# A transformer layer with mixture-of-experts on eight cores: Q/K rotation one head behind the projection, one-queue loads of the layer-norm tiles, and the expert activations loaded four tiles at a time

## The chip, the cores and the metric

The kernel runs on the 8 cores of one Trainium2 chip. Each core computes one of 8 sequences of 2048 tokens with a model width of 2048, and there is no exchange between cores. The metric is the device time in microseconds (us) of the slowest core. Lower is better.

## The reference

One pre-norm transformer layer: x + attention(layernorm(x)), and then that plus a feed-forward part of its layer norm. The part that matters:

```python
q = einsum('bsd,dnh->bsnh', x, wq); k = ...wk; v = ...wv     # 16 heads of 128
q = llama_rope(q); k = llama_rope(k); q = q / sqrt(128)
probs = softmax(where(causal, q @ k.T, -1e30)); attn = probs @ v
x = x + einsum('bqnh,nhd->bqd', attn, wo)
h = einsum('th,ehi->eti', ln(x), w1); g = einsum('th,ehi->eti', ln(x), w3)
y_all = einsum('eti,eih->eth', silu(h) * g, w2)              # 8 experts, inner width 1408
y = sum(y_all of the two best experts * their weights)
shared = silu(ln(x) @ sw1) * (ln(x) @ sw3) @ sw2             # inner width 2816
out = x + y + shared
```

## The kernel before

Every instruction is appended to a list per engine by `emit` (L67), in the order of the Python code, with the semaphores that it waits for. What is given to `p.phase` (L64) is added to the waits of every instruction emitted after it. Engines run their lists in order, so the order of the code is the order of work on each engine. DMAs are issued from three queues: SP (`"sync"`), ACT (`"scalar"`) and POOL (`"gpsimd"`). Between the stages stand barriers (`BAR0`, `BAR1`, `BAR2`, `BAR3`, `BAR3B`, `BAR5A`). All matmul operands are bf16. PSUM is used as two halves, `pA` and `pB`, of 128 x 2048 f32 each. The stages:

- **First layer norm** (L354 to L360): 16 tiles of 128 tokens. `load_xt` (L315) loads a tile `xt` of 128 x 2048 f32 (1 MB) in two halves of 512 KB, the left half from the SP queue and the right half from the ACT queue. There are three tile buffers. `emit_ln` (L293) makes two ACT passes (L294, L297), a few tiny DVE and ACT steps, and one DVE pass (L310); `emit_transposes` (L327) makes 16 PE transposes (L334) and 4 ACT copies (L345) into `XLNT`, the transposed activations. The 8 MB weight `WKV` for K is loaded by POOL from the very start (L279).
- **K and Q projections** (L415 to L456): 32 heads one after another through `proj_head` (L377). For each: 64 matmuls of 512 columns into `pA` (L382); an ACT pass that copies `pA` to `kr` (L389); 4 matmuls with a permutation matrix into `pB` (L393), for the rotary embedding; DVE `t1b` = `kr` x cos (L398), `t2b` = `pB` x sin (L401), the sum `krp` (L403); a store from SP. The phase waits of head n hold the ACT pass and the `t2b` of head n-1, so the matmuls of a head begin when both are over. The weights of Q come per head into two buffers `qc` (L428, L453) from the POOL queue, on which the 8 MB load of V's weight into `WKV` (L431) is issued after the last K head.
- **V projection** (L462 to L484), **attention** (L546 to L650), **output projection** (L674 to L705). The change doesn't touch them.
- **Second layer norm** (L778 to L803): as the first, from `X2_sp` in DRAM, with 16 small gate matmuls per tile (L791), an ACT copy of the gate's logits (L798) and the gate's top-2 chain `gate_chain` (L732), which runs one tile behind: it is emitted between the loads of a tile and its ACT passes.
- **Expert part 1** (L854 to L905): 110 blocks (10 experts `pe`, the last two being the shared one, times 11 blocks `ib` of 128 inner columns), each 64 matmuls into `pA` (L861), 64 into `pB` (L876), ACT silu (L868), DVE products (L889, L891 or L896) into `afin`, and a store of 512 KB to the DRAM tensor `AT_sp` (L901). `AT_sp` is laid out [expert, token tile, ib, 128, 128], so each piece of 256 bytes is separate in DRAM.
- **Expert part 2** (L934 to L991): for each half `dh` of the output columns, each expert and each token tile k (2 x 10 x 16 = 320 tiles), a load of 352 KB `asl` from the ACT queue (L951), 22 matmuls (L958), and a DVE addition to `Yacc` (L968 for the first expert, with the residual `x2b` loaded at L947; L975 for the others). There are four `asl` buffers, and a buffer is loaded again when its tile's matmuls are over. The weight `w2s` (2.8 MB in bf16, read as f32, two buffers) of expert pe+1 is loaded from the POOL queue (L925) once the last tile of expert pe-1 is over. The results go out at L982 with the last expert.

## Time and profile before

| what | us |
|---|---|
| time before, median of 2 runs | 7443.65 (7441.2 to 7446.09) |
| time of the profiled execution | 7449.83 |
| span of its slowest core (core 3), from the first to the last instruction | 7448.3 |
| spans of all cores | 7353.9 to 7448.3 |

The span is the time from the first to the last instruction on the core that took longest; 1.5 us lie around it. Stages are told by their place in the span, in us from its start.

### The profile page before, as it was taken

To read this page: it belongs to the slowest core of one execution; us is meant where nothing else is said; L and a number is where in the kernel's file an instruction comes from. 1 tells how busy PE (TensorE), PEld (TensorE's weight loads), DVE (VectorE), ACT (ScalarE), POOL (GpSimd) and SP (SyncE) were. 2 spreads that over 40 slices of the span, in tenths; PEclk is the share of its full clock that TensorE was granted. 3 is DMA by queue.
4 is the path that set the end of the run, shared out by engine and by line. 5 is a ranking of instruction groups with operands and counts; after the bars stand their busy time and mean duration, and the time that the engine had idled before them with its cause. 6 is when DMAs were issued, how large, how long until landed. Compare 5 with 4: busy or idle time off the path is not lost.

```text
span 7448.3 us, 67106 instructions; the slowest of 8 cores (7353.9 to 7448.3 us)
## 1 busy us (share of the span) xinstructions
PE 6335.2 (85%) x28144; PEld 2705.1 (36%) x28144; DVE 1143.7 (15%) x1337; ACT 1051.4 (14%) x1305; POOL 305.9 (4%) x280
## 2 busy tenths in 40 slices
PE   1477788777766259999999999999999799989999
PEld 0232333111122124444444444444444344434444
DVE  1121210111111211111111111111000122222222
ACT  3200012666600320000000000000000000000000
POOL 0000000000000000000000000000000000000000
PEclk9987898777788579999999999999999899999999
DMA  5104313111144325445455455455554655575655
GB/s 109 42 26 79 48 38 68 34 34 34 27 100 95 88 46 60 55 56 60 52 59 60 52 59 60 54 58 60 55 56 54 140 101 114 108 172 118 119 104 129
DMA packets 1295575, 536.24 MB, mean 72 GB/s; under 512 B 1211424, under 2 KB 1219744, under 8 KB 1295280
## 3 DMA queue, kind: packets, MB, share of 16 engines
q0 software_dynamic: 530896, 207.83, 24.4%
q1 hardware_dynamic: 304096, 191.98, 11.3%
q10 hardware_dynamic: 460288, 132.14, 8.0%
q8 instruction: 228, 3.74, 0.2%
q14 instruction: 67, 0.55, 0.0%
HBM read 623.18 MB, written 116.46 MB: 99 GB/s over the span
## 4 chain that ended last, share of the span: by engine, by line
PE 77%; DMA 13%; ACT 5%; DVE 3%; issue 2%; SPq 0%; DVEq 0%; ACTq 0%; POOL 0%; POOLq 0%
PE pB L876 20%; PE pA L861 20%; PE pA L958 9%; PE pB L958 8%; PE pA L382 7%; DMA asl<-AT_sp 5%; DMA xq<-xin 4%; PE pB L609 3%; PE pB L617 2%; PE pA L583 2%; PE pA L471 2%; DMA xt<-xin 1%; PE pB L471 1%; DVE t2b L401 1%; DMA xt<-X_sp 1%
## 5 line engine op out<-in xcount | busy, mean ns | idle before, releaser
L861 PE MATMUL pA<-XLNT,w1c 128*128 128x512 bf16 x7040 | 1540.9, 380 | 2.1 <-ACT beb L845 2.1
L876 PE MATMUL pB<-XLNT,w3c 128*128 128x512 bf16 x7040 | 1541.8, 380 | 0.0
L876 PEld LDWEIGHTS pB<-XLNT,w3c 128*128 128x128 bf16 x7040 | 689.9, 98 | 835.3 <-issue 9.3
L861 PEld LDWEIGHTS pA<-XLNT,w1c 128*128 128x128 bf16 x7040 | 689.2, 98 | 836.5 <-issue 9.2
L958 PE MATMUL pA<-w2s,asl 128*128 128x512 bf16 x3520 | 810.1, 387 | 105.3 <-DMA asl<-AT_sp 105.3
L958 PE MATMUL pB<-w2s,asl 128*128 128x512 bf16 x3520 | 789.2, 380 | 11.3 <-DMA asl<-AT_sp 11.3
L868 ACT ACTIVATE silu<-pA 128x2048 bf16<-128x2048 f32 x110 | 206.5, 1877 | 2811.8 <-PE pA L861 2756.6
L958 PEld LDWEIGHTS pA<-w2s,asl 128*128 128x128 bf16 x3520 | 348.8, 99 | 543.8 <-issue 148.5
L889 DVE TENSOR_TENSOR atmp<-silu,pB 128x2048 bf16<-128x2048 bf16 x88 | 201.3, 2288 | 2150.0 <-PE pB L876 2125.7
L958 PEld LDWEIGHTS pB<-w2s,asl 128*128 128x128 bf16 x3520 | 345.1, 98 | 429.3 <-issue 18.3
L590 ACT ACTIVATE exp<-pA,EXB 128x512 bf16<-128x512 f32 (+3 forms) x544 | 340.9, 640 | 152.1 <-PE pA L583 147.6
L334 PE MATMUL pA<-IDB,sqb 128*128 128x128 bf16 x256 | 32.4, 306 | 372.2 <-DVE sqb L310 372.2
L382 PE MATMUL pA<-XLNT,qc 128*128 128x512 bf16 x1024 | 260.0, 421 | 61.0 <-DVE t2b L401 41.6
L382 PE MATMUL pA<-XLNT,WKV 128*128 128x512 bf16 x1024 | 260.5, 422 | 49.2 <-DVE t2b L401 39.9
L685 PE MATMUL pA<-woq,ATTNT 128*128 128x512 bf16 x768 | 200.1, 422 | 98.4 <-DVE x2q L692 98.4
L975 DVE TENSOR_TENSOR Yacc<-Yacc,pA 128x1024 f32<-128x1024 f32 x144 | 175.9, 1222 | 598.1 <-PE pA L958 598.1
L583 PE MATMUL pA<-qtn,ktn 128*128 128x512 bf16 (+3 forms) x544 | 219.9, 416 | 53.3 <-DVE ATTNT L644 27.2
L975 DVE TENSOR_TENSOR Yacc<-Yacc,pB 128x1024 f32<-128x1024 f32 x144 | 175.9, 1221 | 511.0 <-PE pB L958 495.5
L609 PE MATMUL pB<-exp,ONESC 128*1 128x512 bf16 (+3 forms) x640 | 240.4, 376 | 2.5 <-DVE exp L597 0.9
L526 POOL DMA_DIRECT2D w1c<-w x88 | 100.8, 1145 | 2215.8 <-PE pA L861 2215.8
L382 PEld LDWEIGHTS pA<-XLNT,qc 128*128 128x128 bf16 x1024 | 107.7, 106 | 216.7 <-issue 123.3
L382 PEld LDWEIGHTS pA<-XLNT,WKV 128*128 128x128 bf16 x1024 | 107.7, 106 | 204.8 <-issue 110.1
(111 smaller groups left out, 2490.6 us busy)
## 6 DMA issues: line engine op xcount, KB each, us to landing
asl<-AT_sp ACTq DMA_DIRECT2D x320, 352.0 KB, 3.6
AT_sp<-afin SPq DMA_DIRECT2D x110, 512.0 KB, 11.7
w1c<-w POOLq DMA_DIRECT2D x88, 512.0 KB, 9.0
w3c<-w POOLq DMA_DIRECT2D x88, 512.0 KB, 13.5
w2s<-w POOLq DMA_DIRECT2D x16, 2816.0 KB, 22.5
xq<-xin SPq DMA_DIRECT2D x64, 256.0 KB, 4.6
X_sp<-x2q SPq DMA_DIRECT2D x64, 256.0 KB, 3.6
x2b<-X_sp SPq DMA_DIRECT2D x32, 512.0 KB, 6.0
```

The costliest lines, as they stand in the source:

```text
L382: emit("tensor", lambda e, db=db, c=c, lcol=lcol, lhs_tile=lhs_tile: e.matmul(pA[:, c * 512:(c + 1) * 512], lhs_tile[:, lcol:lcol + 128], ...
L471: emit("tensor", lambda e, db=db, c=c, ps=ps, i=i: e.matmul(ps[:, c * 512:(c + 1) * 512], XLNT[:, db * 2048 + i * 128: db * 2048 + (i + 1) ...
L583: sps=sps, soff=soff: e.matmul(sps[:, soff:soff + b - a], ktn[par][:, j * 128:(j + 1) * 128], qtn[par][:, q0 + a:q0 + b], start=True, stop ...
L590: sps=sps, soff=soff: e.activation(expt[my_epar][:, 0:b - a], sps[:, soff:soff + b - a], AF.Exp, bias=EXB[:, 0:1]),
L609: stz=first_z[bank], gsp=grp_stop: e.matmul(pB[0:1, a:b], ONESC[:, :], expt[my_epar][:, 0:b - a], start=stz, stop=gsp),
L685: emit("tensor", lambda e, nb=nb, i=i, pcol=pcol, wbuf=wbuf: e.matmul(pA[:, pcol:pcol + 512], ATTNT[:, nb * 2048 + i * 128: nb * 2048 + (i ...
L861: emit("tensor", lambda e, db=db, c=c, slot=slot: e.matmul(pA[:, c * 512:(c + 1) * 512], w1c[slot][:, db * 128:(db + 1) * 128], XLNT[:, db ...
L868: tsilu = emit("scalar", lambda e: e.activation(silu[:, :], pA[:, :], AF.Silu), waits=[th, silu_free], inc="s_s")
L876: emit("tensor", lambda e, db=db, c=c, slot=slot: e.matmul(pB[:, c * 512:(c + 1) * 512], w3c[slot][:, db * 128:(db + 1) * 128], XLNT[:, db ...
L889: ta = emit("vector", lambda e: e.tensor_mul(atmp[:, :], silu[:, :], pB[:, :]), waits=[tg2, tsilu], inc="s_v")
L958: psl=psl: e.matmul(psl[0][:, psl[1] + c * 512: psl[1] + (c + 1) * 512], asl[apar][:, ib * 128:(ib + 1) * 128], w2s[pe % 2][:, ib * 1024 + ...
L975: tac = emit("vector", lambda e, k=k, psl=psl: e.tensor_add(Yacc[k][:, :], Yacc[k][:, :], psl[0][:, psl[1]:psl[1] + 1024]), waits=[tmm, ya ...
```

## The change

It has four parts.

1. `load_xt` issues one DMA of 1 MB for the whole tile, from SP alone. Nothing is issued from ACT any more. It is used in both layer norms.
2. `proj_head` is cut in two, `proj_part` (the 64 matmuls and the ACT pass) and `perm_part` (the permutation, the DVE steps, the store). `perm_part` of head h-1 is emitted after `proj_part` of head h. Even heads use `pA` and odd heads `pB`, and the permutation's result overwrites the half that the head's own projection used. The phase of head h waits for the `t2b` of head h-2. The first two `qc` loads are emitted at the start, and V's weight load after the 64 matmuls of the last K head.
3. `AT_sp` is laid out [expert, ib, 128, token], so a store writes 4 KB rows. Expert part 2 loads four token tiles at once, `aslg` of 128 x 11 x 512 bf16 (1408 KB, in rows of 1 KB), into two buffers; a buffer is loaded again when the fourth of its tiles is over. There are 80 loads in place of 320.
4. The first of these loads and the first `x2b` load are issued before the last expert of part 1.

```diff
     V_sp = nc.dram_tensor("V_sp", [S, D], BF16, kind="Internal")
     X2_sp = nc.dram_tensor("X2_sp", [S, D], F32, kind="Internal")
-    AT_sp = nc.dram_tensor("AT_sp", [NPE, NT, NIB, 128, 128], BF16, kind="Internal")
+    AT_sp = nc.dram_tensor("AT_sp", [NPE, NIB, 128, S], BF16, kind="Internal")
     GSP = nc.dram_tensor("GSP", [8, S], F32, kind="Internal")
 
...
     grb = [A("gr0", [1, S], BF16, offset=WB + 36864),
            A("gr1", [1, S], BF16, offset=WB + 40960)]
 
-    asl = [A("asl0", [128, NIB * 128], BF16, offset=WB + 0),
-           A("asl1", [128, NIB * 128], BF16, offset=WB + 2816),
-           A("asl2", [128, NIB * 128], BF16, offset=WB + 13824),
-           A("asl3", [128, NIB * 128], BF16, offset=WB + 16640)]
-    x2b = [A("x2b0", [128, 1024], F32, offset=WB + 5632),
-           A("x2b1", [128, 1024], F32, offset=WB + 9728)]
+    aslg = [A("aslg0", [128, NIB * 512], BF16, offset=WB + 4096),
+            A("aslg1", [128, NIB * 512], BF16, offset=WB + 15360)]
+    x2b = [A("x2b0", [128, 1024], F32, offset=WB + 0),
+           A("x2b1", [128, 1024], F32, offset=WB + 26624)]
 
 
         def load_xt(i, par, srcten):
             t1 = emit("sync", lambda e, i=i, par=par, srcten=srcten: e.dma_start(
-                xt[par][:, 0:1024], srcten[i * 128:(i + 1) * 128, 0:1024]),
+                xt[par][:, :], srcten[i * 128:(i + 1) * 128, :]),
                 waits=[xt_free[par]], inc=f"l_xt{par}", dma=True)
-            t2 = emit("scalar", lambda e, i=i, par=par, srcten=srcten: e.dma_start(
-                xt[par][:, 1024:2048], srcten[i * 128:(i + 1) * 128, 1024:2048]),
-                waits=[xt_free[par]], inc=f"l_xs{par}", dma=True)
-            return [t1, t2]
+            return [t1]
 
...
+        def proj_part(h, lhs_tile, lhs_kind, n, scale, wtok):
+            par = h % 2
+            ps = pA if par == 0 else pB
             for db in range(ND):
                 lcol = db * 2048 + n * 128 if lhs_kind == "wkv" else db * 128
                 for c in range(4):
-                    emit("tensor", lambda e, db=db, c=c, lcol=lcol, lhs_tile=lhs_tile: e.matmul(
-                        pA[:, c * 512:(c + 1) * 512],
+                    emit("tensor", lambda e, db=db, c=c, lcol=lcol, ps=ps,
+                         lhs_tile=lhs_tile: e.matmul(
+                        ps[:, c * 512:(c + 1) * 512],
                         lhs_tile[:, lcol:lcol + 128],
                         XLNT[:, db * 2048 + c * 512: db * 2048 + (c + 1) * 512],
                         start=(db == 0), stop=(db == ND - 1)),
                         waits=[wtok], inc="s_t")
             tproj = p.tokt("s_t")
-            te = emit("scalar", lambda e, par=par, scale=scale: e.activation(
-                kr[par][:, :], pA[:, :], AF.Copy, scale=scale),
+            TE[h] = emit("scalar", lambda e, par=par, scale=scale, ps=ps: e.activation(
+                kr[par][:, :], ps[:, :], AF.Copy, scale=scale),
                 waits=[tproj], inc="s_s")
...
+        def perm_part(h, n, spill):
+            par = h % 2
+            ps = PSH[h]
             for c in range(4):
-                emit("tensor", lambda e, c=c, par=par: e.matmul(
-                    pB[:, c * 512:(c + 1) * 512], PERMB[:, :],
+                emit("tensor", lambda e, c=c, par=par, ps=ps: e.matmul(
+                    ps[:, c * 512:(c + 1) * 512], PERMB[:, :],
                     kr[par][:, c * 512:(c + 1) * 512], start=True, stop=True),
-                    waits=[te], inc="s_t")
+                    waits=[TE[h]], inc="s_t")
             tperm = p.tokt("s_t")
             t1t = emit("vector", lambda e, par=par: e.tensor_mul(t1b[:, :], kr[par][:, :],
                                                                  COSB[:, :]),
-                       waits=[te, prev_rope], inc="s_v")
-            tv2 = emit("vector", lambda e: e.tensor_mul(t2b[:, :], pB[:, :], SSINB[:, :]),
+                       waits=[TE[h], TROPE.get(h - 1)], inc="s_v")
+            tv2 = emit("vector", lambda e, ps=ps: e.tensor_mul(t2b[:, :], ps[:, :],
+                                                               SSINB[:, :]),
                        waits=[tperm], inc="s_v")
             trope = emit("vector", lambda e, par=par: e.tensor_add(krp[par][:, :], t1b[:, :],
                                                                    t2b[:, :]),
-                         waits=[t1t, tv2], inc="s_v")
+                         waits=[t1t, tv2, TSP.get(h - 2)], inc="s_v")
...
-        ktoks = []
-        for n in range(NH):
-            par = n % 2
-            waits = []
-            if n >= 1:
-                waits += [ktoks[n - 1][0], ktoks[n - 1][1]]
-            if n >= 2:
-                waits += [ktoks[n - 2][2], ktoks[n - 2][3]]
-            p.phase(BAR0 + [cos_tok] + waits)
-            ktoks.append(proj_head(n, WKV, "wkv", KT_sp, 1.0, par,
-                                   p.tokt("w_k"), f"st_kq{par}",
-                                   prev_rope=ktoks[n - 1][2] if n >= 1 else None))
-        t_wv = emit("gpsimd", lambda e: e.dma_start(
-            WKV.ap().rearrange("p (a n) -> p a n", a=16),
-            wv.rearrange("(a p) n -> p a n", p=128)),
-            waits=[TK], inc="w_v", dma=True)
...
+        for h in range(2 * NH):
+            n = h % NH
+            p.phase(BAR0 + [cos_tok] + [t for t in [TV2.get(h - 2)] if t])
+            if h == 0:
+                for m in range(2):
+                    qctoks[m] = emit("gpsimd", lambda e, m=m: e.dma_start(
+                        qc[m % 2].ap().rearrange("p (a c) -> p a c", a=16),
+                        wqr[:, :, m * 128:(m + 1) * 128]), inc=f"w_qc{m % 2}",
+                        dma=True)
+            if h < NH:
+                proj_part(h, WKV, "wkv", n, 1.0, p.tokt("w_k"))
             else:
-                waits += [ktoks[-2 + n][2], ktoks[-2 + n][3]]
-            p.phase(BAR0 + waits)
-            qtoks.append(proj_head(n, qc[par], "qcol", QT_sp, QSCALE, par,
-                                   qctoks[n], f"st_kq{par}",
-                                   prev_rope=(qtoks[n - 1][2] if n >= 1
-                                              else ktoks[-1][2])))
-            if n + 2 < NH:
-                tfree = p.tokt("s_t")
+                proj_part(h, qc[n % 2], "qcol", n, QSCALE, qctoks[n])
+            tfree = p.tokt("s_t")
+            if h == NH - 1:
+                t_wv = emit("gpsimd", lambda e: e.dma_start(
+                    WKV.ap().rearrange("p (a n) -> p a n", a=16),
+                    wv.rearrange("(a p) n -> p a n", p=128)),
+                    waits=[tfree], inc="w_v", dma=True)
+            if h >= NH and n + 2 < NH:
                 qctoks[n + 2] = emit("gpsimd", lambda e, n=n: e.dma_start(
                     qc[n % 2].ap().rearrange("p (a c) -> p a c", a=16),
                     wqr[:, :, (n + 2) * 128:(n + 3) * 128]),
                     waits=[tfree], inc=f"w_qc{n % 2}", dma=True)
+            if h >= 1:
+                hp = h - 1
+                perm_part(hp, hp % NH, KT_sp if hp < NH else QT_sp)
+        perm_part(2 * NH - 1, NH - 1, QT_sp)
         TQV = p.tokt("s_v")
         TQS = p.tokt("s_s")
@@ -851,8 +843,19 @@
         p.phase(BAR3B)
         emit_gate_bcast(0)
         h_free = tbev_pe[0]
+        at0_done = None
+        pre_asl = None
+        pre_x2 = None
         for pe in range(NPE):
             p.phase(BAR3B)
+            if pe == 9:
+                pre_asl = emit("scalar", lambda e: e.dma_start(
+                    aslg[0][:, :].rearrange("p (a c) -> p a c", a=NIB),
+                    AT_sp[0, :, :, 0:512].transpose([1, 0, 2])),
+                    waits=at0_done, inc="l_asl0", dma=True)
+                pre_x2 = emit("sync", lambda e: e.dma_start(
+                    x2b[0][:, :], X2_sp[0:128, 0:1024]),
+                    waits=[beb_use[1]], inc="l_xq0", dma=True)
@@ -899,10 +902,11 @@
                 g_free = tfin
                 silu_free = tfin
                 tsp = emit("sync", lambda e, pe=pe, ib=ib, apar=apar: e.dma_start(
-                    AT_sp[pe, :, ib, :, :].transpose([1, 0, 2]),
-                    afin[apar].ap().rearrange("p (a c) -> p a c", a=16)),
+                    AT_sp[pe, ib, :, :], afin[apar][:, :]),
                     waits=[tfin], inc=f"st_af{apar}", dma=True)
                 afin_free[apar] = tsp
+            if pe == 0:
+                at0_done = [p.tokt("st_af0"), p.tokt("st_af1")]
...
+                    kg, kk = k // 4, k % 4
                     apar = (pe * NT + k) % 4
                     psl = [(pA, 0), (pB, 0), (pA, 1024), (pB, 1024)][apar]
-                    if pe == 0:
+                    if pe == 0 and not (dh == 0 and k == 0):
                         x2tok[k % 2] = emit("sync", lambda e, k=k, dh=dh:
                                             e.dma_start(
                             x2b[k % 2][:, :],
                             X2_sp[k * 128:(k + 1) * 128, dh * 1024:(dh + 1) * 1024]),
                             waits=[x2b_free[k % 2]], inc=f"l_xq{k % 2}", dma=True)
-                    lt = emit("scalar", lambda e, pe=pe, k=k, apar=apar: e.dma_start(
-                        asl[apar][:, :].rearrange("p (a c) -> p a c", a=NIB),
-                        AT_sp[pe, k, :, :, :].transpose([1, 0, 2])),
-                        waits=[aslfree[apar]], inc=f"l_asl{apar}", dma=True)
+                    elif pe == 0:
+                        x2tok[0] = pre_x2
+                    if kk == 0:
+                        cur_ap2 = ((dh * NPE + pe) * 4 + kg) % 2
+                        if dh == 0 and pe == 0 and kg == 0:
+                            cur_lt = pre_asl
+                        else:
+                            cur_lt = emit("scalar", lambda e, pe=pe, kg=kg, dh=dh,
+                                          ap2=cur_ap2: e.dma_start(
+                                aslg[ap2][:, :].rearrange("p (a c) -> p a c", a=NIB),
+                                AT_sp[pe, :, :, kg * 512:(kg + 1) * 512].transpose(
+                                    [1, 0, 2])),
+                                waits=[aslfree[cur_ap2]],
+                                inc=f"l_asl{cur_ap2}", dma=True)
                     for ib in range(NIB):
                         for c in range(2):
-                            emit("tensor", lambda e, ib=ib, c=c, apar=apar, pe=pe,
-                                 psl=psl: e.matmul(
+                            emit("tensor", lambda e, ib=ib, c=c, kk=kk, pe=pe,
+                                 ap2=cur_ap2, psl=psl: e.matmul(
                                 psl[0][:, psl[1] + c * 512: psl[1] + (c + 1) * 512],
-                                asl[apar][:, ib * 128:(ib + 1) * 128],
+                                aslg[ap2][:, ib * 512 + kk * 128:
+                                          ib * 512 + (kk + 1) * 128],
                                 w2s[pe % 2][:, ib * 1024 + c * 512:
                                             ib * 1024 + (c + 1) * 512],
                                 start=(ib == 0), stop=(ib == NIB - 1)),
-                                waits=[lt, ps_free[apar]], inc="s_t")
+                                waits=[cur_lt, ps_free[apar]], inc="s_t")
                     tmm = p.tokt("s_t")
-                    aslfree[apar] = tmm
+                    if kk == 3:
+                        aslfree[cur_ap2] = tmm
                     if pe == 0:
```

On PE, at the start of the projections (`kr` is the copied projection, `PERMB` the permutation matrix, `XLNT` the activations, `WKV` the weight of K; the number behind `kr` is its buffer). Before:

```order
L382 MATMUL pA<-XLNT,WKV 128x512 x64
L393 MATMUL pB<-kr_61,PERMB 128x512 x4
L382 MATMUL pA<-XLNT,WKV 128x512 x64
L393 MATMUL pB<-kr_62,PERMB 128x512 x4
L382 MATMUL pA<-XLNT,WKV 128x512 x64
L393 MATMUL pB<-kr_61,PERMB 128x512 x4
```

and now:

```order
L383 MATMUL pA<-XLNT,WKV 128x512 x64
L383 MATMUL pB<-XLNT,WKV 128x512 x64
L399 MATMUL pA<-kr_61,PERMB 128x512 x4
L383 MATMUL pA<-XLNT,WKV 128x512 x64
L399 MATMUL pB<-kr_62,PERMB 128x512 x4
L383 MATMUL pB<-XLNT,WKV 128x512 x64
L399 MATMUL pA<-kr_61,PERMB 128x512 x4
```

The projection of the next head now stands between a head's projection and its permutation, and the accumulators alternate; the permutation writes where its own head's projection was.

On ACT, at the first two tiles of the first layer norm (`xt` is the loaded tile, `sqb` the work tile). Before:

```order
L319 DMA xt_51<-xin 128x1024
L294 ACTIVATE sqb_54,STATS<-xt_51 128x2048
L297 ACTIVATE sqb_54,STATS<-xt_51 128x2048
L306 ACTIVATE STATS<-STATS 128x1
L308 ACTIVATE STATS<-STATS 128x1
L345 COPY XLNT<-pA 128x4x128 x2
L345 COPY XLNT<-pB 128x4x128 x2
L319 DMA xt_52<-xin 128x1024
L294 ACTIVATE sqb_55,STATS<-xt_52 128x2048
```

and now:

```order
L292 ACTIVATE sqb_54,STATS<-xt_51 128x2048
L295 ACTIVATE sqb_54,STATS<-xt_51 128x2048
L304 ACTIVATE STATS<-STATS 128x1
L306 ACTIVATE STATS<-STATS 128x1
L340 COPY XLNT<-pA 128x4x128 x2
L340 COPY XLNT<-pB 128x4x128 x2
L292 ACTIVATE sqb_55,STATS<-xt_52 128x2048
```

The DMA that stood behind the four copies of a tile and ahead of the next tile's first pass is gone; that pass follows the copies.

On ACT, at the end of expert part 1 and the start of part 2 (`silu` is a block's ACT pass, `asl` and `aslg` the loaded tiles). Before:

```order
L868 ACTIVATE silu<-pA 128x2048 x33
L951 DMA asl_105<-AT_sp 128x11x128
L951 DMA asl_106<-AT_sp 128x11x128
L951 DMA asl_107<-AT_sp 128x11x128
L951 DMA asl_108<-AT_sp 128x11x128
L951 DMA asl_105<-AT_sp 128x11x128
```

and now:

```order
L871 ACTIVATE silu<-pA 128x2048 x22
L852 DMA aslg_105<-AT_sp 128x11x512
L871 ACTIVATE silu<-pA 128x2048 x11
L966 DMA aslg_106<-AT_sp 128x11x512
L966 DMA aslg_105<-AT_sp 128x11x512
L966 DMA aslg_106<-AT_sp 128x11x512
```

The first load stands ahead of the 11 blocks of the last expert. Each of the others brings 128 x 11 x 512 in place of 128 x 11 x 128, and two buffers take turns in place of four.

## Rows read from the trace of the kernel before

**Rows 1.** The page: the chain that ended last, share of the span by engine.
```profile
PE 77%; DMA 13%; ACT 5%; DVE 3%; issue 2%; SPq 0%; DVEq 0%; ACTq 0%; POOL 0%; POOLq 0%
```

**Rows 2.** Windows by stage; columns: stretch and length, engines' busy us, clock, DMA share, GB/s.
```profile
12.00:274.90 262.90, 29.83 (x256) 26.02 (x256) 31.54 (x80) 103.48 (x160) 0.00 (x0) 1.00 0.46 94
283.30:1017.85 734.55, 561.90 (x2177) 226.34 (x2177) 150.37 (x96) 60.07 (x32) 19.44 (x17) 0.83 0.26 45
2446.50:2704.00 257.50, 46.59 (x532) 35.96 (x532) 71.79 (x288) 112.56 (x208) 1.58 (x2) 0.50 0.29 77
2704.00:5776.90 3072.90, 3055.57 (x14109) 1381.18 (x14108) 357.18 (x197) 222.77 (x119) 250.26 (x223) 1.00 0.51 56
5776.90:7448.30 1671.40, 1550.32 (x7041) 693.88 (x7040) 393.15 (x321) 0.00 (x0) 20.13 (x19) 0.97 0.58 123
```

**Rows 3.** Timeline of one tile of the first layer norm: start us, us, engine, line, operation [idle before].
```profile
132.02 1.91 ACT L294 ACTIVATE sqb<-xt 128x2048 bf16<-128x2048 f32 x1 [4.42 <-DMA xt<-xin]
...
141.57 0.62 ACT L345 COPY XLNT<-pB 128x512 bf16<-128x512 bf16 x1
```

**Rows 4.** The window while K's weight is loading (columns as in rows 2), and the first chain pieces.
```profile
24.00:36.00 12.00, 1.86 (x16) 1.62 (x16) 1.97 (x5) 5.40 (x10) 0.00 (x0) 1.00 1.01 186
...
10.67 12.18 DMA xt<-xin
```

**Rows 5.** Timeline of one head of the K projection, columns as in rows 3.
```profile
306.24 16.89 PE L382 MATMUL pA<-XLNT,WKV 128*128 128x512 bf16 x64 [2.55 <-DVE t2b L401]
...
325.25 1.33 PE L393 MATMUL pB<-kr,PERMB 128*128 128x512 bf16 x4 [2.12 <-ACT kr L389]
...
326.69 2.29 DVE L401 TENSOR_TENSOR t2b<-pB,SSINB 128x2048 bf16<-128x2048 f32 x1 [0.18 <-PE pB L393]
```

**Rows 6.** The chain, in order of time: the last DVE step of the Q heads, the second V tile.
```profile
1016.48 1.24 DVE krp L403
...
1033.93 13.81 PE pB L471 x64
```

**Rows 7.** V's weight load (L431, us of its issue), and the timeline's third Q head.
```profile
L431 POOL DMA_DIRECT2D WKV<-wv x1: 1145/1145/1145, 638.9 to 638.9; - x1
...
705.65 16.87 PE L382 MATMUL pA<-XLNT,qc 128*128 128x512 bf16 x64 [19.31 <-DMA qc<-wq]
```

**Rows 8.** Timeline of one tile of the second layer norm, columns as in rows 3.
```profile
2590.48 0.20 ACT L748 ACTIVATE STATS<-STATS 128x1 f32<-128x1 f32 x1
...
2593.40 1.91 ACT L294 ACTIVATE sqb<-xt 128x2048 bf16<-128x2048 f32 x1 [2.72 <-DMA xt<-X_sp]
```

**Rows 9.** Groups by line, expert part 2: busy us, mean ns, idle before and its releaser.
```profile
L958 PE MATMUL pA<-w2s,asl 128*128 128x512 bf16 x3520 | 810.1, 387 | 105.3 <-DMA asl<-AT_sp 105.3
L958 PE MATMUL pB<-w2s,asl 128*128 128x512 bf16 x3520 | 789.2, 380 | 11.3 <-DMA asl<-AT_sp 11.3
```

**Rows 10.** A load in the chain after a change of expert; the timeline's blocks after three waits.
```profile
5895.56 20.66 DMA asl<-AT_sp
...
5916.47 6.78 PE L958 MATMUL pA<-w2s,asl 128*128 128x512 bf16 x22 [6.75 <-DMA asl<-AT_sp]
...
6332.06 6.59 PE L958 MATMUL pA<-w2s,asl 128*128 128x512 bf16 x22 [2.66 <-DMA asl<-AT_sp]
...
6412.38 4.91 PE L958 MATMUL pA<-w2s,asl 128*128 128x512 bf16 x22 [2.50 <-DMA asl<-AT_sp]
```

**Rows 11.** DMA issues: count, KB each, median us to landing.
```profile
asl<-AT_sp ACTq DMA_DIRECT2D x320, 352.0 KB, 3.6
...
w2s<-w POOLq DMA_DIRECT2D x16, 2816.0 KB, 22.5
...
xt<-X_sp ACTq DMA_DIRECT2D x16, 512.0 KB, 3.7
```

**Rows 12.** Timeline of the start of expert part 2.
```profile
5783.40 46.04 ACTq L951 DMA_DIRECT2D asl<-AT_sp  x7
...
5798.31 7.82 PE L958 MATMUL pA<-w2s,asl 128*128 128x512 bf16 x22 [21.37 <-DMA asl<-AT_sp]
```

34 lines of the change are left out of this document (13 added, 21 removed).

## The prediction

> **What bounds the kernel now.** I read the page's chain first, then the windows by stage, then inside three stages the timeline and the groups. The chain is 77% TensorE and 13% DMA [rows 1], so at most a fifth of the span can go without touching the matmuls, and it sits unevenly. In the windows [rows 2] expert part 1 has PE busy for 3055.6 of 3072.9 us at clock 1.00, and nothing in the change can give much there. The first layer norm has PE busy for 29.8 of 262.9 us; the projections have 561.9 of 734.6 us at clock 0.83; the second layer norm 46.6 of 257.5 us; expert part 2 1550.3 of 1671.4 us at clock 0.97. These four are the stages that the change touches. V projection, attention and output projection keep their times.
>
> A full-clock unit for all that follows: 64 matmuls of 512 columns take 13.81 us [rows 6], so one takes 0.216 us, the 4 permutation matmuls 0.86 us, and a tile of 22 in expert part 2 takes 4.75 us.
>
> **First layer norm: -79 us.** ACT does a tile from 132.02 to 142.19, 10.17 us, after having waited 4.42 us for its own half of the load [rows 3], because that half is issued by ACT only among the previous tile's last copies. With all loads on SP, which runs up to three buffers ahead, the wait goes where the DMA can deliver 1 MB in 10.17 us. It can't at first: while K's weight is loading, the DMA engines are full (share 1.01) and write 186 GB/s [rows 4]; if the tile's queue gets half of that, 1.05 MB take 11.3 us. The first tile landed 12.2 us after its issue at 10.7, in two queues of three; in one of two I put it at 26 in place of 22.9. K's weight (8.4 MB at 93 GB/s) is then busy until about 98, so tile i starts at 26 + 11.3 i up to tile 6 (93.8), then nine tiles follow at 10.17 (185.3), and the last ends at 195.5. It ended at 274.9: -79 us. Ends: -89 if the DMA never binds (22.9 + 16 x 10.17 = 185.6), -47 if every tile takes 12.5 us from 28 on.
>
> The Trainium skill ("Trainium Kernel Development and Optimization", Key Constraints) says that DMAs of the SP, ACT and POOL queues share 16 engines, and that issuing from several only saves issue time. By that rule the merged load costs nothing beside K's weight and the first tile stays at 22.9, 3 us better than my sum. No row here shows one queue alone beside the weight.
>
> **Projections: -120 us.** In a head of before, PE stands idle twice: 2.12 us for the ACT pass ahead of the permutation and about 2.6 us for `t2b` behind it [rows 5]. And its 64 matmuls take 16.89 us, not 13.81, since the clock is at 1.2 GHz for a while after these waits. Now the ACT pass lies under the next head's matmuls. The `t2b` stays on the path: head h+1 needs the half that `t2b` of head h-1 is reading, and this is emitted straight ahead of it. So heads 2 to 31 cost 13.81 + 0.86 + 2.6 = 17.3 us, 518 us for 30. The first two have nothing between them: 27.6, and 2.6 more at the start (clock). Whether a single wait of 2.6 us still lowers the clock is open. In expert part 2 a wait of 2.66 us was followed by a block of 6.59 us and one of 2.50 us by a block of 4.91 [rows 10]: 1.7 us or nothing. I take half, 0.85 x 30 = 25.5 (ends 0 and 51).
>
> One stall grows. V's weight was issued at 638.9, and the third Q head, whose weights are queued behind it on POOL, began at 705.65 after 19.31 us of idle time [rows 7], that is 67 us after that issue. The issue is now at the end of the last K head, T; the third Q head could start at T + 38 (three permutations, three waits, two heads) but gets its weights at T + 67: 29 us, and 2 us at the low clock. At the end V waits for the DVE steps of the last two heads, now one after the other: 0.86 + 3.6 + 4.8 + 0.5, some 9.7 us. (DVE's passes are 2.29 for `t2b` and 1.24 each for the other two [rows 5, 6].) The sum is 30.2 + 518 + 25.5 + 31 + 9.7 = 614 us against 734.5: -120 us, ends -146 and -95.
>
> **Second layer norm: -30 us.** Here the next tile's first pass has to wait for the gate's chain too, whose last ACT step ends at 2590.68; the pass started at 2593.40 because of the load [rows 8]. That is 2.7 us in this tile; with the median landing of 3.7 us [rows 11] in place of this one's 4.8 it is 1.6. I take 2.0 for 15 tiles. SP issues a tile's load behind the gate's store of two tiles back, which still leaves about 10 us ahead of its use. Ends -15 and -40.
>
> **Expert part 2: -113 us.** The full-clock work is 320 x 4.75 = 1520 us of 1671.4. PE idles 105.3 + 11.3 = 116.6 us for `asl` [rows 9]; the rest is the low clock after the waits (the block behind the wait of 6.75 us took 6.78 us [rows 10]), the barrier and the tail.
>
> - Start. PE waited 21.37 us, of which the load itself from its issue at 5783.40 was 15 us [rows 12], and 11.3 us for the second tile. With the first group in SBUF, PE starts at the barrier's end, 6.5 us after the last matmul, with 3 us of low clock.
> - The 19 changes of expert, of which 18 are still to be paid with some 84 us of idle time and 20 us of low clock. The loads stall because w2 of the next expert but one (2816 KB, 22.5 us [rows 11]) is issued at the change: a load of 352 KB issued 4.8 us later took 20.66 us, not 3.6 [rows 10, 11], with only 14.25 us (three tiles) to spare. Now the load that falls there is the second group's. It is issued at the change itself, about half a microsecond ahead of w2, and is needed 19.0 us later. It has 128 x 11 = 1408 rows, exactly as many as one old load, each four times as long. Cost from both sides: 3.6 us (as an old load alone) and 27 us (4.8 us of lead gone, the old contended landing of 20.66, and a quarter more bytes per turn of w2's rows, which are 4 KB of source to 1 KB). Starting ahead of w2, it should have about half its rows in before w2's first arrive, so I take 16 us: no stall at most changes.
> - At the changes beside the output stores (`dh` 0, last expert) and beside the `x2b` loads (`dh` 1, first expert) a third stream takes part: 14 us for the two. I add 10 us for short stalls elsewhere, and 5 us of tail.
>
> 6.5 + 3 + 1520 + 14 + 10 + 5 = 1558.5: -113 us. Ends: -137 (nothing but start and tail), and +45 as in the first rival.
>
> The rule that speaks against this part is in the Trainium skill ("DMA: Bandwidth & Descriptors", Queues, rings and completion order): each DMA engine takes turns between its queues, packet by packet. The trace agrees in kind: the small contended load ended with w2, 20.66 us. By that rule the number of rows decides and not their bytes, so a group issued after w2 would take just as long. The same page (Bandwidth) gives 2.0 us + bytes/436 GB/s; by that estimate a group alone takes 5.3 us.
>
> **Expert part 1: 0.** The stores of `AT_sp` were hidden already, PE being busy throughout; the two early loads cost ACT and SP one issue each, and ACT waits for PE most of the time there. If that cover failed, one silu pass would be late once, by less than 1 us.
>
> **Sum.** -79 - 120 - 30 - 113 = -342 us. The profiled execution took 7449.8 us, so 7108; it lies 6.2 us above the median of the runs, so the prediction is 7102 us, 4.6% less than 7443.65.
>
> **The rivals.**
>
> - *Group loads queue behind w2.* If the descriptors of ACT's load don't get ahead of POOL's, the second group of each expert lands 27 us after the change: 8 us of stall and 2 of low clock. For: every load issued in those 22 us was late. Against: the load issued at the change itself didn't stall PE, with 14.25 us to spare. 18 x 10 less the 24 us that I have in: 7102 + 156 = 7258 us. 12%.
> - *The layer norms stay paced by DMA.* If 1 MB on one queue takes as long as the two halves did, the 16.4 us per tile of the first one (262.9/16) stays and the second gains nothing: 7102 + 79 + 30 = 7211. Against: a half alone lands in 3.7 us late on. 5%.
> - *The group load is slow everywhere (slower than before).* Rows of 1 KB out of a DRAM tensor with a 4 KB pitch are not in the trace. All 80 groups need 1.44 MB in 19.0 us, 76 GB/s; each microsecond over it costs 80 us. From 21.4 us on the gain is under 2%, and from 23.3 us (342/80 = 4.3 over) the kernel is slower; at 25 us it takes 7102 + 480 = 7582 us. For: the loads that were contended took 20 us for a quarter of the bytes. Against: w2 brings twice the bytes, out of four times as many in DRAM, in 22.5 us. 2% for slower, and 5% for between, at about 7330 us.
>
> **How the numbers follow.** The forecast has 76%. Its own range from the ends above, not all met at once, is 7045 to 7175. The range for 8 in 10 reaches to the second rival and part of the way to the first: 7045 to 7205. Faster by over 2% (about what a measurement of this kernel tells from no change), which is under 7295 us, holds in the forecast and the first two rivals, 93%; within 2% has 5%, slower 2%.
>
> **What would show it.** In the profile after: the first projection matmul near 204 us and no ACT idle time for `xt` after K's weight is in; an ACT pass per layer-norm tile every 10.2 us and 13.2 us; the projections at about 614 us, with one wait for `t2b` of 2.6 us per head, none for `kr` but at the end, and one for `qc` near 31 us; expert part 2 near 1558 us with hardly any wait for `aslg`. The prediction is wrong if PE waits for `aslg` at most changes of expert, if the clock in the projections stays at 0.83, or if a layer-norm tile still takes over 13 us in the first norm.

## The result, and the profile after

The changed kernel takes 0.951 of the time of the kernel before (95% interval 0.944 to 0.958), which on 7443.65 us is about 7079 us; the prediction was 0.954. The median over all executions is 7221.72 us (11 of them, 7081.64 to 8056.04), above the predicted range, and 7781.65 (10) for the kernel before: in some executions of either kernel the cores of one die or of both are granted a clock near 0.81 for long stretches, for which the prediction's sum has no term, and the ratio and every time and stage length compared below are of executions and cores without that. The profiled execution took 7072.21 us (span 7070.7, on core 1) against 7449.83, so 377.6 us less. The same kernel on another chip gave 0.947 (0.943 to 0.952).

The windows of the kernel after, cut at the same events as [rows 2]: first layer norm, projections, second layer norm, expert part 1, expert part 2. Columns as there.

```profile
12.00:186.00 174.00, 29.84 (x256) 26.05 (x256) 31.54 (x80) 101.89 (x160) 0.00 (x0) 1.00 0.56 142
196.10:796.30 600.20, 489.38 (x2176) 214.26 (x2177) 151.62 (x96) 60.07 (x32) 19.43 (x17) 0.96 0.30 56
2222.70:2449.00 226.30, 46.75 (x532) 35.97 (x533) 71.80 (x288) 112.78 (x209) 1.58 (x2) 0.50 0.30 88
2449.00:5527.80 3078.80, 3063.57 (x14106) 1382.92 (x14107) 357.13 (x197) 220.90 (x118) 250.22 (x223) 0.99 0.44 57
5527.80:7070.70 1542.90, 1528.31 (x7044) 690.40 (x7041) 393.12 (x321) 0.00 (x0) 20.13 (x19) 0.99 0.50 132
```

The first layer norm is 88.9 us shorter at its end (186.0 against 274.9), the projections 134.3 (600.2 against 734.5, and the clock there went from 0.83 to 0.96), the second layer norm 33.5 (226.3, against 259.8 from 2446.5 to before's first matmul of expert part 1 at 2706.3), expert part 2 128.5 (1542.9 against 1671.4). That is 385.2 us, of which 8 are lost in expert part 1, longer on this core by an amount within the spread of the cores of one execution (3063 to 3080 us). V projection and attention kept their times (1009 to 1018 us together on every core). The output projection took 399 us on both of the compared cores; over all cores it varies (375 to 432 us before, 338 to 412 after), and no view here shows by what.

The two cores compared are the slowest of their executions, and in expert part 2 core 3 of before isn't typical. From the last matmul of part 1 to the end the eight cores took 1631 to 1671 us before (core 3 the longest, mean 1642) and 1533 to 1546 after (mean 1541): 100 us less in the mean and not 128.5. The means of the other stages give 84.5 (first layer norm), 130 (projections) and 31 us (second layer norm), which is 346 in all.

The page: the chain by engine (DMA had 13% [rows 1]), the two groups of expert part 2 [rows 9], and of the DMA issues the group loads, the stores of `AT_sp` and w2 [rows 11].

```profile
PE 83%; DMA 7%; ACT 5%; DVE 3%; issue 2%; SPq 0%; DVEq 0%; ACTq 0%; POOL 0%; POOLq 0%
...
L975 PE MATMUL pA<-w2s,aslg 128*128 128x512 bf16 x3520 | 791.6, 381 | 10.2 <-DMA AT_sp<-afin 5.5
L975 PE MATMUL pB<-w2s,aslg 128*128 128x512 bf16 x3520 | 787.6, 380 | 0.0
...
aslg<-AT_sp ACTq DMA_DIRECT2D x80, 1408.0 KB, 8.0
AT_sp<-afin SPq DMA_DIRECT2D x110, 512.0 KB, 7.1
w2s<-w POOLq DMA_DIRECT2D x16, 2816.0 KB, 21.0
```

PE's idle time in expert part 2 fell from 116.6 us to 10.2: 5.5 us of it are the wait at the start, and only 3.4 us are waits for `aslg`. A group of 1408 KB lands in 8.0 us in the median, where I had put 16 at a change of expert.

First layer norm: ACT's timeline at the first tile and, in a second fence, at a tile after K's weight is in (the counterpart of [rows 3]); then the window beside K's weight (the counterpart of [rows 4]).

```profile
23.73 1.91 ACT L292 ACTIVATE sqb<-xt 128x2048 bf16<-128x2048 f32 x1 [12.43 <-DMA xt<-xin]
```
```profile
125.02 1.93 ACT L292 ACTIVATE sqb<-xt 128x2048 bf16<-128x2048 f32 x1
```
```profile
24.00:36.00 12.00, 1.87 (x16) 1.63 (x16) 1.97 (x5) 8.31 (x13) 0.00 (x0) 1.00 1.02 246
```

The bracket for the load is gone from the tile, and while K's weight loads the core moves 246 GB/s, where it moved 186 in [rows 4]. In that window of before, too, the weight had only SP's queue beside it, with rows of 4 KB: ACT issues its half of the second tile at 32.24 us, and its first packets move at 36. So this isn't one queue against two; what the longer rows do of it is measured below.

Projections: the chain, in order of time (a K head at full clock, the DVE step, a head at the low clock after it; further on the `qc` wait), then the list of PE's waits from 190 to 800 us (total us, times, longest).

```profile
264.48 13.97 PE pA L383 x64
...
279.43 2.30 DVE t2b L407
...
281.87 15.66 PE pB L383 x64
...
492.75 45.14 DMA qc<-wq
...
538.03 16.08 PE pA L383 x64
```
```profile
PE pB L383 <- DVE t2b L407: 39.1, 15, 2.7
PE pA L383 <- DVE t2b L407: 36.4, 14, 2.7
PE pA L383 <- DMA qc<-wq: 27.5, 1, 27.5
```

One wait of 2.6 us per head is left, as forecast, and after 6 of these 29 waits the 64 matmuls take 15.66 us in place of 13.97 (granted clock 0.89 over the block, 1.00 otherwise). PE did the same before all of them; the six, at 282, 371, 477, 575, 647 and 736 us, are four to six heads apart. By the windows PE's busy time fell from 561.9 to 489.4 us and its idle time from 172.7 to 110.8: the clock gave 72.5 of the stage's 134 us, and the missing waits the rest.

Expert part 2: the start, and then two issues at a change of expert (ACT's group load by its line, and POOL's w2).

```profile
5533.97 7.60 PE L975 MATMUL pA<-w2s,aslg 128*128 128x512 bf16 x22 [5.49 <-DMA AT_sp<-afin]
```
```profile
L966 ACTq DMA_DIRECT2D aslg<-AT_sp x1: 366/366/366, 5689.5 to 5689.5; - x1
...
5689.99 1.06 POOL L929 DMA_DIRECT2D w2s<-w  x1 [74.92 <-PE pA L975]
```

The 21.37 us of [rows 12] are 5.49. The group goes out 0.5 us ahead of w2 and landed 10.0 us later, w2 itself after 21.1. The slowest group in the chain is one that shares the DMA engines with w2, the output stores and the `x2b` loads, where the second half of the columns begins:

```profile
6319.12 22.98 DMA aslg<-AT_sp
```

### The profile page after: what moved, and what is told of

The parts are those of the page before. It is cut to its first block, busy times and chain, and to the rows that moved or that the text cites. A ratio compares the mean times of both kernels' runs of the same rounds, so it can differ in the third digit from the quotient of the medians.

```text
span 7070.7 us, 66124 instructions; the slowest of 8 cores (6985.6 to 7070.7 us)
## 1 busy us (share of the span) xinstructions
PE 6238.9 (88%) x28144; PEld 2689.3 (38%) x28144; DVE 1144.8 (16%) x1337; ACT 1048.1 (15%) x1305; POOL 305.9 (4%) x280
## 4 chain that ended last, share of the span: by engine, by line
PE 83%; DMA 7%; ACT 5%; DVE 3%; issue 2%; SPq 0%; DVEq 0%; ACTq 0%; POOL 0%; POOLq 0%
PE pB L879 22%; PE pA L864 22%; PE pA L975 11%; PE pB L975 11%; DMA xq<-xin 4%; PE pA L383 3%; PE pB L383 3%; PE pB L601 3%; PE pB L609 2%; PE pA L575 2%; PE pA L463 2%; PE pB L463 2%; DVE t2b L407 1%; ACT sqb L295 1%; ACT sqb L292 1%
## 5 line engine op out<-in xcount | busy, mean ns | idle before, releaser
L879 PEld LDWEIGHTS pB<-XLNT,w3c 128*128 128x128 bf16 x7040 | 691.2, 98 | 843.2 <-issue 21.1
L975 PE MATMUL pA<-w2s,aslg 128*128 128x512 bf16 x3520 | 791.6, 381 | 10.2 <-DMA AT_sp<-afin 5.5
L975 PE MATMUL pB<-w2s,aslg 128*128 128x512 bf16 x3520 | 787.6, 380 | 0.0
L975 PEld LDWEIGHTS pA<-w2s,aslg 128*128 128x128 bf16 x3520 | 345.5, 98 | 431.0 <-issue 24.0
L975 PEld LDWEIGHTS pB<-w2s,aslg 128*128 128x128 bf16 x3520 | 344.8, 98 | 416.5 <-issue 5.1
L589 DVE TENSOR_TENSOR exp<-exp,TRIUB 128x128 bf16<-128x128 bf16 x256 | 57.4, 224 | 716.3 <-ACT exp L582 716.3
L609 PE MATMUL pB<-exp,vn 128*128 128x512 bf16 (+1 forms) x448 | 172.7, 385 | 0.0
L677 PEld LDWEIGHTS pA<-woq,ATTNT 128*128 128x128 bf16 x768 | 77.6, 105 | 219.6 <-issue 151.6
L383 PE MATMUL pA<-XLNT,qc 128*128 128x512 bf16 x512 | 119.0, 396 | 46.1 <-DMA qc<-wq 27.5
## 6 DMA issues: line engine op xcount, KB each, us to landing
w3c<-w POOLq DMA_DIRECT2D x88, 512.0 KB, 10.2
```

What stands on the lines that cost most here:

```text
L383: lhs_tile=lhs_tile: e.matmul(ps[:, c * 512:(c + 1) * 512], lhs_tile[:, lcol:lcol + 128], XLNT[:, db * 2048 + c * 512: db * 2048 + (c + 1) ...
L609: gsp=grp_stop, atps=atps: e.matmul(atps[:, 1024 + a:1024 + b], vn[par][:, j * 128:(j + 1) * 128], expt[my_epar][:, 0:b - a], start=stt, s ...
L677: emit("tensor", lambda e, nb=nb, i=i, pcol=pcol, wbuf=wbuf: e.matmul(pA[:, pcol:pcol + 512], ATTNT[:, nb * 2048 + i * 128: nb * 2048 + (i ...
L879: emit("tensor", lambda e, db=db, c=c, slot=slot: e.matmul(pB[:, c * 512:(c + 1) * 512], w3c[slot][:, db * 128:(db + 1) * 128], XLNT[:, db ...
L975: ap2=cur_ap2, psl=psl: e.matmul(psl[0][:, psl[1] + c * 512: psl[1] + (c + 1) * 512], aslg[ap2][:, ib * 512 + kk * 128: ib * 512 + (kk + 1 ...
```

## The experiments

The stage lengths compared here are the time to the first projection matmul (265 to 291 us over the cores before, 193 to 197 after), the projections (726 to 734, 597 to 603), output projection with second layer norm (645 to 698, 575 to 650) and expert part 2 from its first matmul (1613 to 1650, 1528 to 1541).

**One part of the change at a time.** Three kernels, each the kernel before with one part of the diff shown above.

*The layer-norm loads alone (part 1 of the change).*

```diff
-                xt[par][:, 0:1024], srcten[i * 128:(i + 1) * 128, 0:1024]),
+                xt[par][:, :], srcten[i * 128:(i + 1) * 128, :]),
                 waits=[xt_free[par]], inc=f"l_xt{par}", dma=True)
-            t2 = emit("scalar", lambda e, i=i, par=par, srcten=srcten: e.dma_start(
-                xt[par][:, 1024:2048], srcten[i * 128:(i + 1) * 128, 1024:2048]),
-                waits=[xt_free[par]], inc=f"l_xs{par}", dma=True)
-            return [t1, t2]
+            return [t1]
```

> Only the one-queue loads of the layer-norm tiles, in the kernel before. My theory (each part of the change acts on its own stage alone): first layer norm from 263 to about 174 us, second from 258 to about 226, all other stages as before, in total 122 us less than the kernel before. Rival (the parts lean on one another, because earlier or later stages shift the cores' DMA against each other): a layer norm within 20 us of its old length, or a total gain under 80 us.

Measured: 196 to 198 us to the first projection matmul (82 less in the mean of the cores), and 233 to 240 us from the last matmul of the output projection to the first of expert part 1 (265 to 273 before, 32 less in the mean; output projection included it is 587 to 662). On the cores at full clock the projections took 730 to 731 us and expert part 2 1622 to 1640, as before. The slowest core took 7474.9 us at the least, with a clock of 0.913; the twelve cores with a mean clock of 0.925 or more took 7272 to 7333 us, 7300 in the mean, where the fifteen of the kernel before on the same chip took 7345 to 7483, 7411 in the mean. That is 111 us less, where 122 were expected and the rival had under 80. The two terms are this part's and depend on no other.

*The rotation alone (part 2).*

```diff
-        def proj_head(n, lhs_tile, lhs_kind, spill, scale, par, wtok, stsem,
+        def proj_part(h, lhs_tile, lhs_kind, n, scale, wtok):
...
+        def perm_part(h, n, spill):
```

> Only the rotation one head behind, in the kernel before. My theory: projections from 734 to about 600 us, clock of that stage about 0.96 in place of 0.83, one wait for the third Q head's weights near 28 us, total gain about 134 us. Of that, 68 us are the idle time for the kr copy, some 40 us the clock. Rival (the shorter stage only runs into V's weight load): V's first tile waits for its weight, and less than 100 us are gained in total.

Measured: 7323.4 and 7377.0 us against 7487.9 (one execution) on the same chip; projections 600.5 to 604 us, 128 less in the mean, and the other stages as before (expert part 2 1622 to 1667, two cores somewhat over those of before).

*The groups and the two early loads alone (parts 3 and 4).*

```diff
-    AT_sp = nc.dram_tensor("AT_sp", [NPE, NT, NIB, 128, 128], BF16, kind="Internal")
+    AT_sp = nc.dram_tensor("AT_sp", [NPE, NIB, 128, S], BF16, kind="Internal")
...
+                        cur_ap2 = ((dh * NPE + pe) * 4 + kg) % 2
```

> Only the new layout, the loads of four tiles and the two early loads, in the kernel before. My theory: expert part 2 from 1671 to about 1543 us, waits for the activations under 10 us, total gain about 128 us. Rival (the cores are less in step here than with the shorter layer norms, so w2 and the group loads meet otherwise): waits of several us at some changes of expert, stage over 1580 us.

Measured: 7326.8 and 7338.5 us against 7487.9; expert part 2 1539 to 1552 us, 5.8 us of wait at its start (91 less in the mean, the wait included), expert part 1 unchanged. By the means over the cores, the parts' stage gains (114, 128 and 91) add up to 333 us, where the whole change has 346 in the same stages: none of them takes from another, and 10 of the 13 us between are expert part 2, somewhat shorter in the whole (1541 against 1551).

**The kernel after without its two early loads.**

```diff
-            if pe == 9:
-                pre_asl = emit("scalar", lambda e: e.dma_start(
...
-                    if pe == 0 and not (dh == 0 and k == 0):
+                    if pe == 0:
```

> The changed kernel without the two early loads: the first group and the first x2b are loaded after the barrier. My theory: PE waits for the first group as it waited for the first asl, about 15 us longer at the start of expert part 2, and nothing else changes: stage about 1543 + 15 to 25 = 1560 to 1568 us. Rival (the early loads only move the wait, since the second group and w2 then come late together): stage within 5 us of 1543.

The runs took 7859 us and more, so only the stage lengths of the cores at full clock are read. The timeline of PE on core 2, at the start of expert part 2:

```profile
6066.76 6.62 PE L963 MATMUL pA<-w2s,aslg 128*128 128x512 bf16 x22 [28.82 <-DMA aslg<-AT_sp]
```

PE waited 24 to 30 us here, where the kernel after waits 5.5; from that first matmul on, part 2 takes 1535 to 1541 us on cores 2 to 5, as with the early loads. So the early loads are worth 18 to 24 us, and the groups the rest. (Groups without early loads start later than the kernel before did, which waited 18 to 21 us: the first load is four times as large.)

**What a queue's turn is: two DMAs of 4 KB rows from SP in place of one of 8 KB rows.** My term had given the tile half of the traffic beside K's weight. A single queue did better; was that the queue or the row?

```diff
-            t1 = emit("sync", lambda e, i=i, par=par, srcten=srcten: e.dma_start(
-                xt[par][:, :], srcten[i * 128:(i + 1) * 128, :]),
-                waits=[xt_free[par]], inc=f"l_xt{par}", dma=True)
+            for hf in range(2):
+                t1 = emit("sync", lambda e, i=i, par=par, srcten=srcten, hf=hf: e.dma_start(
+                    xt[par][:, hf * 1024:(hf + 1) * 1024],
+                    srcten[i * 128:(i + 1) * 128, hf * 1024:(hf + 1) * 1024]),
+                    waits=[xt_free[par]], inc=f"l_xt{par}", dma=True)
```

> The changed kernel with each layer-norm tile loaded by two DMAs of rows of 4 KB, both from SP, in place of one DMA of rows of 8 KB. Theory A (a queue gets one row per turn, so 8 KB rows got the tile two thirds of the bytes beside K's weight and 4 KB rows get it half): while K's weight is loading a tile takes about 11.3 us in place of 10.1, the first pass starts near 26 to 28 us in place of 23.7, and the windows show about 186 GB/s in place of 246. Theory B (the queues share bytes, or the load alone has room): first pass near 23.7, 10.1 us per tile throughout.

The timeline of ACT on core 0, the first passes of two tiles, and the window beside K's weight:

```profile
27.03 1.91 ACT L292 ACTIVATE sqb<-xt 128x2048 bf16<-128x2048 f32 x1 [16.70 <-DMA xt<-xin]
...
38.12 1.91 ACT L292 ACTIVATE sqb<-xt 128x2048 bf16<-128x2048 f32 x1 [1.02 <-DMA xt<-xin]
```
```profile
24.00:36.00 12.00, 1.63 (x16) 1.63 (x16) 1.98 (x5) 5.37 (x8) 0.00 (x0) 1.00 1.02 221
```

First tile at 27.0, the next 11.1 us later, 221 GB/s in place of 246, and 202 to 207 us to the first projection matmul; the run took 7098.8 us. These are my 26 and 11.3 us. Bytes, queue and issuer are the same; the rows are half as long, and there are two DMAs to a tile. The packets tell which of the two counts. The DMA view of the same window, by queue (q0 is POOL's with the weight, q1 SP's with the tiles: packets, MB, share), first of the kernel after, then of this one:

```profile
q0 software_dynamic: 264, 1.08, 54.6%
q1 hardware_dynamic: 256, 1.88, 47.6%
```
```profile
q0 software_dynamic: 340, 1.39, 69.4%
q1 hardware_dynamic: 339, 1.25, 32.1%
```

One row is one packet, and in both kernels the two queues move about one packet each in turn. With 8 KB rows the tile gets 63% of the bytes, with 4 KB rows 47%. (The weight's rows are 4 KB as they land; some 30 packets of each q1 are of 4 bytes.) So it is the rows: the queues take turns row by row.

**Where ACT issues its half.** The kernel before with its two halves, but ACT's half issued ahead of the previous tile's passes.

```diff
+            if i + 1 < NT:
+                tr = load_xr(i + 1, (i + 1) % 3, xin)
             tx = emit_ln(xt[par], sqb[bpar], lts, sq_waits=[sq_free[bpar]])
```

> The kernel before, still with two halves from two queues, but ACT issues its half for tile i+1 ahead of the passes of tile i. Theory A (what cost time was the place of the issue in ACT's order, not the second queue): first layer norm near 175 to 185 us after K's weight has its share, second near 226, as with one queue. Theory B (one DMA of 1 MB in rows of 8 KB is needed): the second norm gains, but the first stays over 200 us because 4 KB rows get half the turns beside K's weight.

ACT's timeline on core 0, the issue and the pass of the following tile behind it:

```profile
122.23 0.33 ACTq L321 DMA_DIRECT2D xt<-xin  x1
...
122.85 1.94 ACT L294 ACTIVATE sqb<-xt 128x2048 bf16<-128x2048 f32 x1
...
132.91 1.94 ACT L294 ACTIVATE sqb<-xt 128x2048 bf16<-128x2048 f32 x1
```

The 4.42 us of [rows 3] are gone, the tile takes 10.06 us, the first projection matmul comes at 201 to 206 us, and output projection with second layer norm is 633 to 665 us; the run took 7385.0 us. So 76 of the first term's 84.5 us (means over the cores), and the second term with it, come from the place in ACT's order. The 9 us that are left are lost while K's weight loads, where every other tile takes some 13 us. They aren't shown to be the rows' doing: the first pass starts at 23 to 25 us, as in the kernel after (22 to 24), for two queues of 4 KB rows get two turns to the weight's one (from 36 to 42 us of the kernel before the three queues moved 82, 81 and 86 packets). But ACT issues its half only one tile ahead, and SP its own up to three, and no run separates this from the rest.

**What holds up the group loads.** In the kernel after, the group load is issued 0.5 us ahead of w2. Three kernels change the rows or the moment.

*Rows of 256 B.* The layout of `AT_sp` of before, each group brought by four DMAs into the same buffer: the same bytes, 5632 rows in place of 1408, and the 320 DMAs of before.

```diff
-    AT_sp = nc.dram_tensor("AT_sp", [NPE, NIB, 128, S], BF16, kind="Internal")
+    AT_sp = nc.dram_tensor("AT_sp", [NPE, NT, NIB, 128, 128], BF16, kind="Internal")
...
+                            for q in range(4):
+                                cur_lt = emit("scalar", lambda e, pe=pe, kg=kg, q=q,
+                                              ap2=cur_ap2: e.dma_start(
```

> The changed kernel with the activations of part 1 in the layout of before (rows of 256 bytes), each group of four tiles loaded by four DMAs of 1408 rows into the same two buffers, issued together at the same moments. Theory A (beside w2 it is the number of rows that counts): 5632 rows instead of 1408 don't get in ahead of w2; the group lands near w2's end, 24 to 28 us after the change, PE waits 5 to 9 us at each change and expert part 2 grows by 100 to 200 us. Theory B (what helped is only that a load of a larger block is asked for 19 us ahead): no waits, stage near 1540 us.

The chain's piece after a change of expert, and PE's timeline there:

```profile
5665.10 26.77 DMA aslg<-AT_sp
```
```profile
5692.12 6.49 PE L980 MATMUL pA<-w2s,aslg 128*128 128x512 bf16 x22 [10.93 <-DMA aslg<-AT_sp]
```

Expert part 2 takes 1708 to 1730 us, some 180 more than in the kernel after and some 80 more than in the kernel before, its wait at the start included; the run took 7289.0 us. Asking for a larger block earlier isn't enough. The DMA view from 5670 to 5683 us, with both loads under way (q0 w2, q10 the group):

```profile
q0 software_dynamic: 882, 1.81, 91.6%
q10 hardware_dynamic: 880, 0.23, 12.9%
```

Row for row again: a row of 256 B takes a turn as one of 1 KB does, so four times the rows need four times the turns. The number of DMAs was changed with the rows, and the last two of the four are issued 0.7 and 2.4 us behind w2; what that adds isn't separated.

*Issued 6.1 us later.* The load also waits for the addition of four tiles back.

```diff
-                                waits=[aslfree[cur_ap2]],
+                                waits=[aslfree[cur_ap2], tac_hist[-4]],
```

> The changed kernel with each group load issued only when the first tile of the group before it has been added, about 6.3 us later than in the changed kernel, so that at a change of expert w2's load is in its full course (12.7 us of lead are left). Theory A (one row per turn, so it is the number of rows that counts beside w2, and 1408 rows take as long as an old load behind w2 did, 16 to 21 us): it lands about 23 to 27 us after the change, PE waits 4 to 8 us at each change and expert part 2 grows by 100 to 180 us. Theory B (bytes share): four times the bytes of an old contended load, over 40 us to land, waits over 25 us. Theory C (no contention that matters for rows of 1 KB): lands in under 12 us, no waits.

PE's waits in expert part 2, core 5:

```profile
PE pA L976 <- DMA aslg<-AT_sp: 118.2, 19, 17.0
```

Expert part 2 takes 1681 to 1686 us on cores 4 to 7, some 147 more. The contended group is issued 5.7 us behind w2 and lands about 17 us after its issue, 23 after the change. It has 1408 rows, as one old load had, which was issued 4.3 us behind w2 and took 20.66 us [rows 10] with a quarter of the bytes.

*Issued 1.4 us later.* The buffer is released by the DVE addition in place of the matmuls.

```diff
-                    if kk == 3:
-                        aslfree[cur_ap2] = tmm
...
+                    if kk == 3:
+                        aslfree[cur_ap2] = tac
```

> The changed kernel with a group buffer released by the DVE addition of its fourth tile and not by its matmuls, so that the group load is issued about 1.6 us later, some 1 us behind w2's issue on POOL instead of half a microsecond ahead. My first rival (descriptors behind w2's): it lands over 22 us after the change and PE waits 5 us or more each time. My theory (w2's rows begin to move 3 us after its issue, so the group still has 1 to 2 us alone): landing at the changes 12 to 17 us in place of 8 to 11, no waits, stage within 10 us of 1540.

I had expected no waits from so small a delay. The timeline of core 7 at a change of expert, the chain's piece, the next PE block that needs the group, and PE's waits in part 2:

```profile
5622.87 1.06 POOL L929 DMA_DIRECT2D w2s<-w  x1 [77.63 <-PE pA L975]
5623.80 0.37 ACTq L966 DMA_DIRECT2D aslg<-AT_sp  x1
```
```profile
5623.80 21.33 DMA aslg<-AT_sp
```
```profile
5645.38 4.85 PE L975 MATMUL pA<-w2s,aslg 128*128 128x512 bf16 x11 [4.06 <-DMA aslg<-AT_sp]
```
```profile
PE pA L975 <- DMA aslg<-AT_sp: 89.6, 17, 15.4
```

Expert part 2 takes 1652 to 1675 us, some 130 more; the run took 7196.9 us. That expectation fell. Issued 0.5 us ahead of w2 the group lands in 10.0 us (7.2 to 11.8 at the changes without another stream); issued 0.9 us behind it, in 21.3 us, as long as w2 itself (22.0). The DMA view shows both courses. First the kernel after, from the group's issue to just before w2's first row (5689.9 to 5695.27 us), and from 5695.5 to 5699 us; then this kernel from 5627 to 5643 us:

```profile
q10 hardware_dynamic: 1085, 1.11, 68.1%
```
```profile
q0 software_dynamic: 275, 0.56, 84.5%
q10 hardware_dynamic: 273, 0.27, 27.6%
```
```profile
q0 software_dynamic: 1218, 2.49, 82.3%
q10 hardware_dynamic: 1217, 1.25, 28.2%
```

With the group in front, 1085 of its 1408 rows are in before w2's first row moves, 5.3 us after w2's issue; only the rest has to take turns. With w2 in front, w2's first row moves 1.8 us after its issue and the group's first one 2.6 us after its own; from there each row of the group waits for a row of w2. Both have 1408 rows, so they end together. There is hardly anything between the two courses, and the whole gain of the groups hangs on this order: behind w2 the stage, with its wait at the start, takes 1670 us in the mean, 28 more than in the kernel before.

**V's weight in pieces.** The largest wait left outside the heads is the 27.5 us for `qc`, whose load stands on POOL behind V's weight. V's weight in eight pieces between the `qc` loads:

```diff
             if h == NH - 1:
-                t_wv = emit("gpsimd", lambda e: e.dma_start(
-                    WKV.ap().rearrange("p (a n) -> p a n", a=16),
-                    wv.rearrange("(a p) n -> p a n", p=128)),
-                    waits=[tfree], inc="w_v", dma=True)
+                load_wv(0, [tfree])
...
+                if n < 7:
+                    load_wv(n + 1, [])
```

> The changed kernel with V's weight loaded in eight pieces of 1 MB (bf16), one behind the last K head and one behind each of the first seven loads of Q weights. My theory (the 27.5 us wait of the third Q head is only the place of its weights behind the 61 us load in POOL's queue): the wait goes, projections from 600 to about 572 us, 28 us less in all, 0.4% below the changed kernel. Rival (the DMA engines are the limit there, so the Q weights come late wherever they stand): waits of several us at several Q heads or at V's first tile, and under 10 us gained.

> The changed kernel again, on the same chip as the one with V's weight in pieces. Both theories: about 7079 us, 0.951 of the kernel before, expert part 2 near 1540 us.

> V's weight in eight pieces once more, to time it against the kernel before: the projections took 574 us in place of 601 in its first profile. My theory: 0.947 of the kernel before (near 7055 us), 0.4% below the changed kernel. Rival (what is gained there is lost at the next barrier): 0.951, as the changed kernel.

The projections of the version with eight pieces by windows (core 5), and PE's waits there:

```profile
193.00:768.00 575.00, 488.45 (x2176) 213.99 (x2176) 150.88 (x96) 60.06 (x32) 24.14 (x24) 0.98 0.30 58
```
```profile
PE pA L383 <- DVE t2b L407: 39.1, 15, 2.7
PE pB L383 <- DVE t2b L407: 39.1, 15, 2.7
```

The wait for `qc` isn't in the list any more, and the projections take 573 to 575 us against 598 to 605 of the kernel after on the same chip. The version with eight pieces took 7061.6 and 7049.1 us where the kernel after took 7084.9 to 7099.3 (four executions); in a repetition on another chip 7054.6 and 7092.3, with projections of 573.5 to 574.6 on the six cores at full clock. The stage's 27 us are shown twice; for the total there are two executions of this version on each chip and no interval, so that the 0.4% is likely and not proved.

## What the prediction had right, and which of its terms were mis-sized

The measured ratio, 0.951, lies 0.3% below the forecast's 0.954, and each of the four stages gained for the reason given. What failed is the size of terms, all to the same side: the four stages gained 385 us on the compared cores, where the sum has 342. The largest two are the low clock in the projections ("I take half", 25.5 us; measured 10) and, in expert part 2, the group beside w2 ("about half its rows", "I take 16 us", and 29 us for what remains; measured 1085 of 1408 rows, 10.0 us, and 14). By the steps of the prediction:

- **First layer norm, -79 forecast, -88.9 measured.** The mechanism held (no wait for `xt` once K's weight is in; 9.9 to 10.4 us per tile). Mis-sized was "if the tile's queue gets half of that": the queue gets half of the turns, which with 8 KB rows is 63% of the bytes. The first tile came at 23.7 and not 26, and no tile took 11.3 us. The run with 4 KB rows gives 27.0 and 11.1, so the sum was right for rows as long as the weight's. The weight was in at 85 us and not at 98. "No row here shows one queue alone beside the weight" is a misreading: the window of [rows 4] is just that, with 4 KB rows (310 packets of the weight, 267 of SP's queue, none of ACT's). The end I gave for a DMA that never binds (-89) is what was met. The Trainium skill's rule ("Trainium Kernel Development and Optimization", Key Constraints), that several queues only save issue time, gave 22.9 us for the first tile, and the trace's 23.7 agrees. By itself it doesn't give the time: the same bytes on the same queue in shorter rows came at 27.0.
- **Projections, -120 forecast (614 us), -134 measured (600.2).** 29 waits of 2.6 us for `t2b` and one of 27.5 us for `qc` (29 forecast, with 2.1 us of low clock behind it, 2 forecast) are as reckoned; so is the tail, 9.7 us. Mis-sized was "I take half": the low clock follows 6 of 29 waits, at 1.7 us each, 10 us and not 25.5. The heads cost 17.4 to 17.5 us, for 17.3. Of the kernel before, "its 64 matmuls take 16.89 us" holds for every other head only: most heads alternate between about 16.8 and 15.6 us. The sum doesn't use it.
- **Second layer norm, -30 forecast, -33.5 measured.** The pass now stands straight behind the gate's last ACT step: 

```profile
2346.29 0.20 ACT L740 ACTIVATE STATS<-STATS 128x1 f32<-128x1 f32 x1
2346.40 1.89 ACT L292 ACTIVATE sqb<-xt 128x2048 bf16<-128x2048 f32 x1
```

  where 2.72 us stood between them [rows 8]; 2.2 us per tile rather than 2.0.
- **Expert part 2, -113 forecast (1558.5 us), -128.5 measured (1542.9).** The start is as forecast: 6.2 us to the first matmul, and a first block of 7.60 us, 2.9 more than at full clock. Of the 29 us allowed for the busy changes, short stalls and tail, 14 were used. "I take 16 us" for a group at a change was too long, 7.2 to 11.8 us; its lead over w2 was worth 1085 of 1408 rows and not "about half its rows", but with 19.0 us to spare 16 would have cost nothing either. The 1671.4 us against which the gain was reckoned are those of core 3, 30 more than the mean of the cores; the gain in the mean, 100 us, lies below the forecast's 113. The length was forecast too long, and the reference was too long as well.
- **Expert part 1, 0 forecast.** The stage stays within the cores' spread, as said.
- **The rivals.** None came. But the first one, group loads behind w2, had the right mechanism and nearly the right price: I gave 156 us and a landing of 27, and the kernel with a delay of 1.4 us shows 130 us and 23 us after the change. What I put at 12% is decided by half a microsecond of issue order. That order could be read before: at each change one `asl` load goes out 0.5 to 0.8 us ahead of w2 and, past the start, lands in 3.2 to 6.3 us. How thin the margin is couldn't. The Trainium skill's turns packet by packet ("DMA: Bandwidth & Descriptors", Queues, rings and completion order) agree with the packets of all these kernels: 880 rows of 256 B beside 882 of w2, 1217 of 1 KB beside 1218, 339 of 4 KB beside 340 of K's weight. In these runs a turn is one row, whether of 256 B, 1, 4 or 8 KB.
- **Slips that move nothing.** The end of expert part 2 "as in the first rival" is +43 us and not +45, and a range up to 7205 doesn't quite reach the second rival's 7211.

The forecast erred to the same side in all four stages, by 10, 14, 4 and 15 us, since each unknown was taken between its ends and each landed near the good one. In the two profiled executions the sum was 342 us against 377.6.

## What to carry to other kernels

Where a load competes with a bulk transfer, its rows decide and not its bytes: make them as long as the layout allows, and put the urgent load's issue ahead of the bulk one's, by construction and not by the half microsecond that it happens to have. A load that is issued from a compute engine starts only when that engine comes to it in its order; ask of each such issue what stands ahead of it. When an urgent small load stands behind a large one on the same queue, cut the large one into pieces between the small ones.

## What the runs showed of the hardware that I had not expected

- Beside an 8 MB weight load (rows of 4 KB as they land), a queue with 8 KB rows brought the core's traffic to 246 GB/s, and the same queue with the same bytes in 4 KB rows to 221: the queues moved 264 and 256 packets in the one case, 340 and 339 in the other, and a packet is a row.
- A group issued 0.5 us ahead of w2 landed after 10.0 us, 0.9 us behind it after 21.3 us. w2's own first row moved 1.8 us after its issue when it came first, and 5.3 us when the group did. The order of two issues within 1.5 us was worth 130 us over the changes of expert of part 2.
- The same wait of 2.6 us left the clock at 2.4 GHz in 23 cases of 29 and brought it to 1.2 GHz for part of the next block in 6 (15.66 us in place of 13.97). In the kernel before, with two waits per head, the clock fell in every head behind the first: the blocks took 15.3 to 17.7 us.
